# An eight-layer transformer stack on one core: norm statistics taken in the layer that last adds to x, and the normalising shared by two engines

## The reference, cut to what matters

```python
def _layernorm(x, axis=-1, eps=1e-05):
    m = jnp.mean(x, axis=axis, keepdims=True)
    v = jnp.var(x, axis=axis, keepdims=True)
    return (x - m) / jnp.sqrt(v + eps)
```

## Time and profile before

| what | value |
|---|---|
| median of three runs | 1294.65 us |
| the profiled execution, its own time | 1300.77 us |
| its span, first to last instruction | 1299.1 us |
| TensorE matmuls busy | 981.3 us, 76% |
| VectorE busy | 746.6 us, 57% |
| ScalarE busy | 565.4 us, 44% |
| GpSimd busy | 335.5 us, 26% |
| mean granted TensorE clock | 0.859 of 2.4 GHz |

### The profile page before, as it was taken

The page is one execution under the profiler, slowest core; times in us unless marked ns, Lnnn a source line. Parts: engine busy times, 40 slices in busy tenths (PEclk is TensorE's granted clock), DMA queues, the critical chain, the costliest instruction groups (busy, mean ns, idle before and its releaser), DMA issues. The chain is left out here.

```text
span 1299.1 us, 26809 instructions
## 1 busy us (share of the span) xinstructions
PE 981.3 (76%) x10797; PEld 639.1 (49%) x10825; DVE 746.6 (57%) x2078; ACT 565.4 (44%) x914; POOL 335.5 (26%) x364
## 2 busy tenths in 40 slices
PE   2899698998999968986960908854656865689966
PEld 1477433443334326774850906633535644446656
DVE  2476657545556555534552332484999999336652
ACT  2365265544554435533620504671555444145430
POOL 2330200000000015762015552462332332213330
PEclk9799689999999979996975858995779877689987
DMA  6000000000000000004201311000000000000000
GB/s 248 1 2 2 18 1 0 1 1 0 1 0 1 1 1 2 3 3 190 74 2 47 94 43 65 2 1 1 2 2 3 3 1 3 1 2 2 3 1 33
DMA packets 14569, 27.77 MB, mean 21 GB/s; under 512 B 1008, under 2 KB 12272, under 8 KB 13552
## 3 DMA queue, kind: packets, MB, share of 16 engines
q1 hardware_dynamic: 13424, 23.97, 5.1%
q0 software_dynamic: 1024, 2.10, 0.6%
HBM read 20.17 MB, written 5.90 MB: 20 GB/s over the span
## 5 line engine op out<-in xcount | busy, mean ns | idle before, releaser
L1171 PE MATMUL l0f_ctl<-l1f_in,l0f_in 128*128 128x512 f32 x320 | 147.9, 606 | 0.5
L456 DVE TENSOR_REDUCE l_neg_max<-l_scores 128x8 f32<-128x1024 f32 x64 | 78.4, 1225 | 96.2 <-PE l_scores L318 96.2
L2341 ACT COPY l2f_blocks_sb<-l2f_right_t_sb 32x1024 f32<-32x1024 f32 x64 | 66.8, 1043 | 92.8 <-DVE l2f_right_t_sb L2457 91.7
L419 ACT ACTIVATE l_probs<-l_scores 128x1024 f32<-128x1024 f32 x64 | 65.6, 1024 | 81.6 <-PE l_scores L324 81.6
L1171 PEld LDWEIGHTS l0f_ctl<-l1f_in,l0f_in 128*128 128x128 f32 x320 | 62.5, 195 | 73.0 <-issue 71.7
L318 PE MATMUL l_scores<-l_k_heads,l_q_all 32*128 32x256 f32 x512 | 78.8, 427 | 8.3 <-POOL l_k_heads L266 3.8
L164 POOL TENSOR_SCALAR l_ln_var_eps<-l_ln_mean_var 128x8 f32<-128x8 f32 x8 | 2.1, 256 | 311.7 <-DVE l_ln_mean_var L146 311.7
L324 PE MATMUL l_scores<-l_q_all,l_k_heads 32*128 32x128 f32 x1024 | 75.8, 287 | 1.5 <-ACT l_probs L419 1.5
L572 POOL TENSOR_TENSOR l_sim_squares<-l_sim_exps 128x1024 f32<-128x1024 f32 x32 | 60.6, 1895 | 27.3 <-ACT l_sim_exps L686 27.3
L2251 PE MATMUL l2f_sim_ps<-l1f_in,xnT 128*128 128x512 f32 x32 | 28.9, 1008 | 47.9 <-DVE l1f_in L2425 47.2
L318 PEld LDWEIGHTS l_scores<-l_k_heads,l_q_all 32*128 32x128 f32 x512 | 49.0, 199 | 32.8 <-issue 31.1
(11 more groups left out here) (425 smaller groups left out, 2446.1 us busy)
## 6 DMA issues: line engine op xcount, KB each, us to landing
l1f_in<-in_l1f SPq DMA_DIRECT2D x1, 4580.0 KB, 14.7
l0f_in<-in_l0f SPq DMA_DIRECT2D x1, 2302.5 KB, 8.9
l1f_in<-in_l2u SPq DMA_DIRECT2D x1, 2048.0 KB, 7.9
sorted_rows<-common_in SPq DMA_DIRECT2D x1, 1856.0 KB, 10.6
l0f_in<-in_l2f SPq DMA_DIRECT2D x1, 1792.5 KB, 19.4
l1f_sorted<-sorted_rows SPq DMA_DIRECT2D x7, 256.0 KB, 4.6
expert_rows<-l1f_y SPq DMA_DIRECT2D x7, 256.0 KB, 2.3
x_in<-in_x SPq DMA_DIRECT2D x1, 1024.0 KB, 4.9
```

The lines of the kernel that those rows point to most:

```text
L419: nc.scalar.activation(probs[c % 2][:, 2 * pair:2 * pair + 2], scores2[:, :, :, :, :], ACT.Exp, scale=SCORE_SCALE).then_inc(exp_done, 1)
L456: V.tensor_reduce(out, scores1[:, :, :, :, :].rearrange("p g j t s -> p (g j) t s"), AX.X, ALU.max, negate=True).then_inc(max_taken, 1)
L1171: return nc.tensor.matmul(out, lhs, rhs, start=start, stop=stop)
L2341: A.copy(blocks[rows, :, u, :], right_t[rows, :, :]).then_inc(blocks_made, 1)
```

## The change

- Every layer but the last takes the statistics of a batch, or of four, on VectorE right behind its last add to x, into tensors that all layers share. In the attention layers with one batch a round they come one round later. At the end of its block GpSimd waits for 12 batches and computes their rstd.
- The norm block has 12 batches' rstd at its start. GpSimd makes `away` = -mean x rstd for them and the rstd of the last four. ScalarE normalises batches 3, 7 and 11 as scale x + bias; VectorE normalises the other 13. There are four PSUM tiles in place of two, and no wait for one to come free.
- With the RMS gain the two norms are one formula: variance times (1 + 1e-6) plus 1e-11, then one power.
- The first norm takes its own statistics in four groups of four. It waits only for x and a small new load (`first`: identity and -0.5); SyncE waits for the others and issues the four later loads in the norm's own block.

```diff
+class RowStats:
+    KNOWN = 12
+    def take(self, dve, first, last):
+        m = self.m
+        for b in range(first, last):
+            self.nc.vector.bn_stats(m["row_stats"][:, b, :], m["x"][:, b, :]).then_inc(self.measured, 1)
+        dve.wait_ge(self.measured, last)
+        for b in range(first, last):
+            self.nc.vector.bn_aggr(m["row_mean_var"][:, b, :], m["row_stats"][:, b, :]).then_inc(self.combined, 1)
+
+    def scale(self, pool, first, last, rms=False, step=1):
+        m, h = self.m, slice(first, last)
+        grow, eps = (1.0 + RMS_EPS, RMS_EPS * LN_EPS) if rms else (1.0, LN_EPS)
+        self.nc.gpsimd.tensor_scalar(m["row_var_eps"][:, h], m["row_mean_var"][:, h, 1], grow, eps, ALU.mult, ALU.add) \
+            .then_inc(self.eps_added, 1)
+        pool.wait_ge(self.eps_added, step)
+        return self.nc.gpsimd.tensor_tensor(m["row_rstd"][:, h], m["row_var_eps"][:, h], m["minus_half"][:, h], ALU.pow)
+
+    def scale_known(self, pool, rms=False):
+        pool.wait_ge(self.combined, self.KNOWN)
+        self.scale(pool, 0, self.KNOWN, rms)
...
+def layernorm(nc, m, tag, known=RowStats.KNOWN, rms_gain=None, keep=None, meanwhile=None):
...
+        mine = [b for b in range(known) if b % 4 == 3]
...
         @block.vector
         def _(dve):
...
+            if not known:
+                for i in range(NCH):
+                    row_stats.take(dve, 4 * i, 4 * i + 4)
+            for b in range(B):
+                if b in mine:
+                    continue
+                if b >= known and b in (known, 8):
+                    dve.wait_ge(rstd_made, 1 + [first for first, _ in late].index(b))
+                nc.vector.tensor_scalar(xn[:, b, :], x[:, b, :], m["row_mean_var"][:, b, 0:1], m["row_rstd"][:, b:b + 1],
+                                        ALU.subtract, ALU.mult).then_inc(xn_made, 1)
 
         @block.gpsimd
         def _(pool):
...
+            if known:
+                nc.gpsimd.tensor_tensor(away[:, 0:known], m["row_mean_var"][:, 0:known, 0], m["row_rstd"][:, 0:known],
+                                        ALU.mult).then_inc(away_made, 1)
+                pool.wait_ge(away_made, 1)
+                nc.gpsimd.tensor_scalar(away[:, 0:known], away[:, 0:known], -1.0, None, ALU.mult).then_inc(away_made, 1)
+            for n, (first, last) in enumerate(late):
+                if not known:
+                    pool.wait_ge(row_stats.combined, last)
+                row_stats.scale(pool, first, last, rms=rms_gain is not None, step=n + 1).then_inc(rstd_made, 1)
...
         @block.scalar
         def _(act):
...
+            def normalise(b):
+                nc.scalar.activation(xn[:, b, :], x[:, b, :], ACT.Identity, scale=m["row_rstd"][:, b:b + 1],
+                                     bias=away[:, b:b + 1]).then_inc(turned_in, 1)
+
+            if known:
+                act.wait_ge(away_made, 2)
+            for b in mine[:2]:
+                normalise(b)
+            for i in range(NCH):
+                act.wait_ge(xn_flipped, 4 * i + 4)
...
+                if i == 0:
+                    for b in mine[2:]:
+                        normalise(b)
...
@@ cross_attention, at the end of a round of VectorE
+                if exists(b - 5):
+                    dve.wait_ge(added, b - 4)
+                    row_stats.take(dve, b - 5, b - 4)
...
@@ attend_tempered
-            for c in range(B + 3):
+            for c in range(B + 4):
...
+                if exists(c - 4):
+                    dve.wait_ge(added, c - 3)
+                    row_stats.take(dve, c - 4, c - 3)
...
@@ refine_experts, finish
+                work.wait_freed(dve, name, 0)
+                row_stats.take(dve, 4 * c, 4 * c + 4)
...
@@ top1_experts
+                dve.wait_ge(added, 4 * i + 4)
+                row_stats.take(dve, 4 * i, 4 * i + 4)
...
@@ two_attentions, add
+                dve.wait_ge(added, c + 1)
+                row_stats.take(dve, 4 * c, 4 * c + 4)
...
@@ product_keys, add
+                wait_freed(dve, use)
+                row_stats.take(dve, GB * g, GB * g + GB)
...
@@ build
-                load(sp, "x", "common", "l0", "ctxT", *[n for n in m if n in dram and n not in ALONE])
-                wait(sp, "x", "common")
-                wait(sp, "l0", "ctxT", *[n for n in m if n in dram and n not in ALONE])
-                load(sp, "l0f", "l1", "l2", "l3f")
+                load(sp, "x", "first", *others)
+                wait(sp, "x", "first")
+
+        def rest(sp):
+            wait(sp, *others)
+            load(sp, "l0f", "l1", "l2", "l3f")
```

More of the change, by code:

```diff
@@ L124, in layernorm @@
[L124 removed]
+        xn = keep
         if keep is None:
[L126 to L133 removed]
@@ L139, in _ @@
+        row_stats = RowStats(nc, m, new_semaphore, tag)
+        rstd_made, xn_made, xn_flipped, xnT_stored = sem("rstd_made"), sem("xn_made"), sem("xn_flipped"), sem("xnT_stored")
+        away_made, turned_in = sem("away_made"), sem("turned_in")
+        block = ctx.enter_context(nc.Block())
+        late = [(known, B)] if known else [(0, 8), (8, B)]
+        @block.sync
+        def _(sp):
+            if meanwhile is not None:
+                meanwhile(sp)
         @block.vector
         def _(dve):
-            for half in range(2):
-                for b in range(half * 8, half * 8 + 8):
-                    nc.vector.bn_stats(stats[:, b, :], x[:, b, :]).then_inc(stats_made, 1)
-                dve.wait_ge(stats_made, half * 8 + 8)
-                for b in range(half * 8, half * 8 + 8):
-                    nc.vector.bn_aggr(mean_var[:, b, :], stats[:, b, :]).then_inc(aggregated, 1)
@@ L202, in cross_attention @@
+def cross_attention(nc, m, w, tag, meanwhile, masked_keys=False, causal=False, first=None):
+    if first is None:
+        layernorm(nc, m, tag + "_ln")
+    else:
+        layernorm(nc, m, tag + "_ln", known=0, meanwhile=first)
     x, xnT, ctxT, identity = m["x"], m["xnT"], m["ctxT"], m["identity"]
@@ L882, in _ @@
                     .then_inc(bo_added, 1)
+            row_stats.scale_known(pool)
         @block.tensor
@@ L2560 @@
 ALONE = ("x", "ctxT")
+FIRST = ("identity", "minus_half")
 def group_of(name):
     tag = name.split("_")[0]
-    return tag if tag in GROUPS else "common"
+    return tag if tag in GROUPS else "first" if name in FIRST else "common"
 def pack(arrays):
@@ L2658, in _layout_ffn, with build @@
     out["l2u_up"] = np.tile(a["L2_ffn_expert_up"].reshape(32, 32, P), (4, 1, 1))
-LAYERS = ("l0_xattn", "l0_ffn", "l1_xattn", "l1_ffn", "l2_xattn", "l2_ffn", "l3_xattn", "l3_ffn")
 IN_PLACE_OF = {"l2f": "l0f", "l2u": "l1f", "l3": "l0"}
-def build(nc, dram, where, out, layers=LAYERS):
+def build(nc, dram, where, out):
     with ExitStack() as ctx:
@@ L2681, in build @@
             loaded[n] = ctx.enter_context(nc.semaphore(n + "_loaded"))
-            if n not in GROUPS and n != "common":
+            if n not in GROUPS + ("common", "first"):
                 m[n] = group[n]
-        by_group = {g: {} for g in GROUPS + ("common",)}
+        by_group = {g: {} for g in GROUPS}
         for name, (g, first, shape) in where.items():
@@ L2722, in wait @@
                 sp.wait_ge(loaded[n], 16)
+        others = ["common", "l0", "ctxT"] + [n for n in m if n in dram and n not in ALONE]
         with nc.Block() as block:
@@ L2740, in build @@
         ]
-        if layers != LAYERS:
-            first = [r[2] for r in run if r[0] == layers[0]][0]
-            with nc.Block() as block:
-                @block.sync
-                def _(sp):
-                    if first in IN_PLACE_OF:
-                        wait(sp, IN_PLACE_OF[first])
-                        load(sp, first)
-                    wait(sp, first)
         for name, layer, tag, options, meanwhile in run:
-            if name in layers:
-                layer(nc, m, by_group[tag], tag, meanwhile if layers == LAYERS else (lambda sp: None), **options)
+            layer(nc, m, by_group[tag], tag, meanwhile, **options)
         with nc.Block() as block:
```

109 lines of the change are left out of this document (41 added, 68 removed).

## The result

The changed kernel took 1263.52 us in the median of four runs (1256.24 to 1265.29), the kernel before, on the same chip, 1295.22 (1293.15 to 1296.31): a ratio of 0.9747, 95% interval 0.9705 to 0.9788. It is faster by 31.7 us; the prediction had 1262 and 1250 to 1271. The profiled execution took 1265.29 us with a span of 1263.6, against 1300.77 and 1299.1 before, so the two traces differ by 35.5 us.

The account below looks back on a forecast made before the run. The prediction took the norms, run in series between layers, as paid in full. Savings of 30.9, 10.75 and 7.9 less 16.7 paid in the layers gave 32.8 us off the 1294.65 median: 1262, range 1250 to 1271.

Parts of the forecast that it names:

- Norms in series, paid in full: Eight norms, each a block between two layers: no layer work runs beside a norm, so its length is paid in full.
- A: Seven later norms: six fall from 9.96 to 4.8 us, saving 30.9; the RMS norm saves 10.75.
- B: Start and first norm: end moves from 25.38 to 17.5 us, saving 7.9, bounds 5 and 9.
- C, attention rounds at nothing: Layers l0, l1, l3: one-batch statistics of 0.45 us fit in VectorE's idle time of 0.50, 1.12 and 0.95 a round.
- C, l0_ffn 4.4: l0_ffn's four statistics groups: 1.3 us each for chunks 1 and 2, 1.3 at the end, 0.5 for chunk 0.
- C, l1_ffn 1.3: l1_ffn: three statistics groups hide in gather waits, the last pays 1.3 us; GpSimd's power ends before VectorE.
- C, l2_xattn and l2_ffn: Statistics cost 3.9 us in l2_xattn (chunks 0, 1, 3) and 4.4 in l2_ffn (1.3 each, chunk 2 0.5).
- The lock: VectorE's tensor_scalars and GpSimd's power do not stop each other: the eight-column power took 1.67 us either way.
- Rival 1: Shorter TensorE idle at norms keeps 2.4 GHz in layers: 20 us in full, 1242, half 1252; chance 0.15.
- the granted clock at 1.0 where a layer starts: At the start of a layer: listed among the signs that would show the prediction wrong.
- Rivals 2 to 5: Statistics overflow attention rounds: 1272, chance 0.08; late power: 1270, 0.05; l1 loses clock: 1310, 0.02; second load late: 1268, 0.05.
- Rival 4: l1's rounds: statistics lose TensorE's clock, a 3.28 us round grows by up to 3, 48 rounds by over 100; chance 0.02.

Follow-up runs that it names:

- e4: Changed kernel's layers with statistics and power unused, but norms and start of the kernel before: 1313.00 us, ratio 1.0147 to the kernel before.
- e11: The changed kernel again with no edit, beside later runs: 1264.22 us, ratio 0.9756 to the kernel before.
- e9: Changed kernel with l0_ffn's statistics of a finished chunk, except the last, held until VectorE has written the next x_next: 1254.68 us, ratio 0.9664.
- e2: The kernel before with only the new start (small first load, other loads awaited beside the first norm): 1284.70 us, ratio 0.9930.
- e8: Changed kernel with l1_ffn's GpSimd power over 12 batches moved to the head of l2's norm: 1258.06 us, ratio 0.9725.
- e10: Changed kernel with the edit of e9, and l2_xattn's statistics of chunks 1 and 2 held until ahead of the last add: 1257.61 us, ratio 0.9711.
- e1: The changed kernel again with no edit: 1260.41 us, ratio 0.9754 to the kernel before.
- e7: Changed kernel with eight unread matmuls added in each of seven norms, four ahead of the transposes and four behind: 1264.81 us, ratio 0.9781.

## Why the prediction was right, point by point

- **Norms in series, paid in full.** Right: what left the norm stretches left the time.
- **A, 30.9 for six norms and 10.75 for the RMS norm.** Right. 4.89 us from first instruction to last copy against 4.8; l2_ffn's norm 4.89 (866.04 to 870.93) against the 15.65 of the earlier trace rows. The working had TensorE catch up with VectorE at the tail; it ends 0.84 behind VectorE's last operation, where the earlier trace rows has 0.53: the 16 transposes keep it busy for 3.86 us, longer than VectorE's 3.42. That is the 0.1.
- **B, 7.9.** It gave 8.75, within its bounds. Two terms were too dear: a group of four statistics takes 1.17 here (6.42 to 7.63 is 1.21, 7.63 to 8.79 is 1.16) and not the 1.31 of the earlier trace rows, which includes a memset; and the second power ends at 13.29, about when VectorE asks for it (11.13 + 8 x 0.27 = 13.3), so VectorE waits only 0.08 us for it.
- **C, attention rounds at nothing.** Right: 72.1 us from first to last add in l0, before, after and in e4, and its later rounds are 5.21 us as before. Of the 0.50 us of the earlier trace rows nothing is left. The timeline of the changed kernel in that round:

```profile
115.50 0.29 DVE L120 BATCH_NORM_STATS2 row_stats<-x_in 128x6 f32<-128x128 f32 x1
115.82 0.18 DVE L123 BATCH_NORM_AGGREGATE row_mean_var<-row_stats 128x2 f32<-128x6 f32 x1
116.08 1.23 DVE L481 TENSOR_REDUCE l_neg_max<-l_scores 128x8 f32<-128x1024 f32 x1
```

- **C, l0_ffn 4.4.** Right in mechanism, a little low: 3.4 inside (3.1 forecast), and 1.3 at the end. Chunk 0's add costs nothing (0.5 was taken); the two x_next waits cost 1.2 and 1.2 (the fifth x_next stands 31.1 behind the fourth in e11 and 29.9 in e9, the eighth 32.4 behind the seventh and 31.2), and 0.6 to 0.7 lies in the interval between the fifth and the sixth, 29.8 in the changed kernel's first trace and 30.0 in e11 against 29.3 in e9. The kernel before has 31.3 in the first of these intervals where e2 has 29.8, so its trace alone would hide the first wait; the total is 258.2 and 258.4 in the two.
- **C, l1_ffn 1.3: the term that was wrong.** The sum took GpSimd's power to be hidden behind VectorE. "Ends near 773.8, before VectorE's 775.1": GpSimd's power did end before VectorE, by 1.4 us, and still the block ended 1.26 us late, as e8 shows. The boundary costs 2.55 (e4), not 1.3. B's term was 0.85 too small the other way, so the sum doesn't show the miss.
- **C, l2_xattn and l2_ffn.** Right, in l2_xattn by the very chunks that were named (the adds stand 4.85, 4.12 and 3.55 apart instead of 3.64, 2.80 and 3.55): 2.5 for 2.6 and 2.7 for 2.6 to 3.1, plus the 1.3 at each end (1.0 and 1.3 measured).
- **The lock.** GpSimd's power of four columns took 1.04 us beside the 13 tensor_scalars, and over eight columns 1.70 at the start beside them: no hold, as the sum had it. In e10 it is otherwise beside VectorE's additions of two SBUF buffers: 2.71 instead of 2.31 for twelve columns, and the short operation 0.55 instead of 0.20. The Trainium skill, SBUF — State Buffer, "Who interferes with whom", says that a VectorE instruction with two inputs in SBUF contends with a GpSimd one that reads it; these two rows agree. The rule that the prediction held against its rows, one instruction kept waiting for the whole of the other, isn't seen in the norms' tensor_scalars, but the kernel before shows it elsewhere, so "do not stop each other" holds for the pair in the norms and not for every pair. The timeline of the kernel before in l2_xattn, GpSimd's addition of two buffers and VectorE's tensor_scalar of four columns, which takes 0.17 in the earlier trace rows:

```profile
855.74 1.26 POOL L1942 TENSOR_TENSOR l_res_sb<-l_res_sb,l_last_b_sb 128x512 f32<-128x512 f32 x1
855.85 1.18 DVE L2116 TENSOR_SCALAR l_neg_mean_sb<-l_mean_var_sb 128x4 f32<-128x4 f32 x1
```

  It ends with GpSimd's. What sets the two pairs apart no run here shows.
- **Rival 1, the clock stays up.** Its sign was seen, its gain was not shown. In the seven later norms the granted clock is still 0.50 to 0.66. But at the first matmul of the seven later layers it stands at 1.00 in three, five and three of them in the changed kernel's first trace, e1 and e11, against one in the kernel before, one in e2 and two in e4; "the granted clock at 1.0 where a layer starts" was a sign that the prediction named against itself. It doesn't last: in l0_ffn it is back at 0.50 from 143.8 to 150.6 in the first trace. From first matmul to first add the eight layers together take 664, 652 and 655 us in these three traces, against 665 and 659 in the kernel before and e2, so a gain of some microseconds can't be excluded, and the 20 of the full form can. Inside the layers TensorE spends 298 us at 1.2 GHz in the changed kernel's first trace and 270 in e1's and in e11's, against 283 in that of before and 261 in e2's. The scatter within one kernel is as large as the difference between these kernels. The Trainium skill, TensorE: Matmul & The Clock Gate, "What's actually happening", has the rate follow the engine's recent work; e7, which gives it more, gets faster transposes and has 1.00 at the first matmul of all seven layers, so the trace agrees, but it gets no shorter run.
- **Rivals 2 to 5.** None came: rounds as long as before, GpSimd not named as releaser of VectorE's operations in any of the seven later norms, l1's rounds at 3.28, x landing in time for 6.42. (Rival 4's price was too high: the round of 3.28 us is l1's alone, 16 rounds and not 48.)
- **The sum.** 32.8 was foretold and the traces differ by 35.5. 32.5 of it can be put down to the change, by the table: 41.3 gained less 8.8 paid. The remaining 3.0 lies in stretches that differ by as much between two executions of one kernel; whether a small form of rival 1 is in it stays open. The medians agree to 1.5 us, where the twelve runs of the changed kernel spread over 11 and two terms were wrong by 0.85 and 1.25 in opposite directions: that closeness is luck.

## What to carry to other kernels

Where stages run one behind the other, work moved out of a boundary pays in full there, and costs in its new place only where it stands in a chain that somebody waits for: put it behind the instruction that another engine is waiting for (e9), not behind the last one that it needs. When the clock scatters a run by more than the term in question, compare traces between two milestones of the same engine beyond the stretch in which the clock comes back, look at the same stretch in a second trace of each kernel, and only then at the totals. An engine may not be free for the end of a block when its last row ends: behind indirect loads, look at when the next block begins.
